# Routing stage of a fused decoder layer: token weights, placing matmuls and low halves in another order

## The reference

```python
scores = jax.nn.sigmoid(x @ gate_w.T) + bias
topk_w, topk_idx = jax.lax.top_k(scores, TOPK)                     # 4 of 16 experts
topk_w = topk_w / (jnp.sum(topk_w, axis=-1, keepdims=True) + 1e-20)
...
z = jax.nn.silu(g) * u                                             # g, u: x by Wg, Wu of each expert
out = jnp.einsum('eti,ehi->th', zw, Wd)                            # zw: z by the token's weight
out = out + jax.nn.silu(x @ Sg.T) * (x @ Su.T) @ Sd.T              # the shared expert
```

## Time and profile before

| | us |
|---|---|
| median of 3 runs | 1754.04 |
| lowest and highest | 1752.56 and 1755.8 |
| profiled execution | 1757.54 |
| its span | 1755.7 |

### The profile page before, as it was taken

The page is one execution under the profiler, slowest core; times in us unless marked ns, Lnnn a source line. Parts: engine busy times, 40 slices in busy tenths (PEclk is TensorE's granted clock), DMA queues, the critical chain, the costliest instruction groups (busy, mean ns, idle before and its releaser), DMA issues. The chain is left out here.

```text
span 1755.7 us, 39041 instructions
## 1 busy us (share of the span) xinstructions
PE 1689.7 (96%) x15461; PEld 964.6 (55%) x15461; DVE 1267.1 (72%) x2051; ACT 919.4 (52%) x1518; POOL 958.2 (55%) x875
## 2 busy tenths in 40 slices
PE   7899998899999999999999999999899999999997
PEld 4666664455555555555555555555455555455553
DVE  6778776778888888888888888888785444344445
ACT  6776674656464645455555545565643333233334
POOL 5556664556464636465555555464634555455544
PEclk9999999899999999999999999999999999999999
DMA  5431223112212314122222122131266778877658
GB/s 163 133 86 39 74 62 80 61 58 88 70 64 72 109 43 142 46 100 93 72 73 97 37 97 73 37 109 37 77 226 216 145 146 224 241 190 151 116 97 299
DMA packets 88897, 190.68 MB, mean 109 GB/s; under 512 B 14800, under 2 KB 33744, under 8 KB 86672
## 3 DMA queue, kind: packets, MB, share of 16 engines
q1 hardware_dynamic: 65232, 130.72, 22.3%
q0 software_dynamic: 22912, 57.32, 16.0%
q10 hardware_dynamic: 576, 0.14, 0.0%
HBM read 124.95 MB, written 63.21 MB: 107 GB/s over the span
## 5 line engine op out<-in xcount | busy, mean ns | idle before, releaser
L1136 POOL TENSOR_TENSOR xa_sc<-xa_sc,xa_rs 128x1024 f32<-128x1024 f32 x32 | 60.8, 1901 | 375.4 <-DVE xa_rs L1396 375.4
L1125 POOL TENSOR_TENSOR xa_xs<-xa_xs,sn 128x512 f32<-128x512 f32 x160 | 233.7, 1460 | 46.3 <-ACT xa_xs L1177 46.3
L288 PE MATMUL bank<-xhl,front_h 128*128 128x512 f16 x640 | 244.4, 382 | 11.3 <-DVE front_l L670 10.0
L289 PE MATMUL bank<-xhl,front_h 128*128 128x512 f16 x640 | 244.3, 382 | 0.0
L290 PE MATMUL bank<-xhl,front_l 128*128 128x512 f16 x640 | 244.1, 381 | 0.0
L1130 POOL TENSOR_TENSOR xa_rr<-xa_x,xa_xs 128x512 f32<-128x512 f32 x160 | 232.2, 1451 | 12.7 <-DVE xa_x L1287 0.2
L2042 POOL DMA_INDIRECT scratch_y<-raw_front,moe_to x79 | 125.3, 1585 | 149.5 <-DVE mo_zl L2096 121.5
L288 PE MATMUL bank<-out_h,xa_oh 128*128 128x512 f16 x512 | 194.8, 381 | 10.2 <-DVE xa_ol L1269 8.0
L289 PE MATMUL bank<-out_l,xa_oh 128*128 128x512 f16 x512 | 194.7, 380 | 0.0
L290 PE MATMUL bank<-out_h,xa_ol 128*128 128x512 f16 x512 | 194.5, 380 | 0.0
L1176 ACT ACTIVATE xa_xs<-bank 64x512 f32<-64x512 f32 x160 | 95.0, 593 | 139.3 <-PE bank L290 124.4
(11 more groups left out here) (320 smaller groups left out, 4668.8 us busy)
## 6 DMA issues: line engine op xcount, KB each, us to landing
xa_rawc<-in_ew SPq DMA_DIRECT2D x32, 768.0 KB, 5.4
moe_ring<-scratch_w SPq DMA_DIRECT2D x16, 1536.0 KB
scratch_w<-xa_chunk_h SPq DMA_DIRECT2D x32, 384.0 KB, 2.3
scratch_w<-xa_chunk_l SPq DMA_DIRECT2D x32, 384.0 KB, 3.3
raw_front<-in_xwq SPq DMA_DIRECT2D x8, 1024.0 KB, 7.9
raw_out<-in_xwo SPq DMA_DIRECT2D x8, 1024.0 KB, 5.3
scratch_y<-acc SPq DMA_DIRECT2D x6, 1024.0 KB, 7.8
acc<-in_x POOLq DMA_DIRECT2D x4, 1024.0 KB, 7.2
```

What stands on the lines that cost most here:

```text
L288: pe.matmul(out_ap, ah, bh, start=start and m == 0, stop=False)
L289: pe.matmul(out_ap, ah, bl, start=False, stop=False)
L1125: PO.mark(pool.tensor_tensor(xr, xr, sn[:, :].rearrange("p (a s) -> p a s", a=1) .to_broadcast([P, QT // S, S]), ALU.mult), f"sm{r}", st)
L1136: PO.mark(pool.tensor_tensor(s4, s4, rs[:, :, :].rearrange("p h (t a) -> p (h t) a", a=1) .to_broadcast([P, 16, S]), ALU.mult), "nm", st)
```

## The change

- The four operations that make `w4` move from in front of the use of the counts to behind the first four groups of comparisons, in front of `z1.0` and `z1.1`.
- TensorE's order behind `counts` was: `gu1.0`, `gu1.1`, place 0 to 3, `y0.0`, place 4 to 7, `owners`, `y0.1`, `y0.2`, `y0.3`. It becomes: `gu1.0`, `y0.0`, `y0.1`, then `gu1.1` with one placing matmul behind each of its 24 wide ones, the 8 that are left of groups 0 to 3, then `y0.2` and `y0.3` with one placing matmul of groups 4 to 7 behind each of their 12 wide ones, the 20 that are left, and `owners`. The rest (`y1.0`, `y1.1`, `turn0` and so on) is as before.
- The low halves `zl1.0` and `zl1.1` of quarter 1 are no longer made by GpSimd ahead of its wait for the list, but by VectorE behind `list` and in front of `tables`.

The number of matmuls is the same. In `front_with_places` and `back` the three products of `three_pass` are written out one by one. The diff, shortened:

```diff
--- before.py
+++ after.py
@@ -1642,14 +1642,14 @@
             assert PLACES == 8
 
             PE = Timeline(sem("ro_pe"), [], 0,
-                          ["logits"] + quad("gu", 0, IB) + ["counts"] + quad("gu", 1, IB) + several("place", *range(4)) + ["y0.0"]
-                          + several("place", *range(4, 8)) + ["owners", "y0.1", "y0.2", "y0.3", "y1.0", "y1.1", "turn0", "y1.2", "turn1", "y1.3"])
+                          ["logits"] + quad("gu", 0, IB) + ["counts", "gu1.0", "y0.0", "y0.1", "place0", "place1", "gu1.1", "place2", "place3", "y0.2", "place4",
+                                                                "y0.3"] + several("place", *range(5, 8)) + ["owners", "y1.0", "y1.1", "turn0", "y1.2", "turn1", "y1.3"])
             shared_act = [f"{w}{q}.{n}" for q in range(2) for w in ("si", "zh") for n in range(IB)]
             AC = Timeline(sem("ro_act"), [], 0, ["sig"] + shared_act + quad("y", 0, TQ) + ["y1.0", "y1.1", "xh0", "y1.2", "xh1", "y1.3"])
             DV = Timeline(sem("ro_dve"), [], 0,
-                          ["down", "chosen"] + quad("z", 0, IB) + ["w4", "slots"] + several("at", *range(4)) + quad("z", 1, IB)
-                          + several("at", *range(4, 8)) + ["own", "list", "tables", "to", "xl0", "xl1", "ws0", "ws1"])
-            PO = Timeline(sem("ro_pool"), [], 0, [x for q in range(2) for x in quad("zl", q, IB)])
+                          ["down", "chosen"] + quad("z", 0, IB) + ["slots"] + several("at", *range(4)) + ["w4"] + quad("z", 1, IB)
+                          + several("at", *range(4, 8)) + ["own", "list"] + quad("zl", 1, IB) + ["tables", "to", "xl0", "xl1", "ws0", "ws1"])
+            PO = Timeline(sem("ro_pool"), [], 0, quad("zl", 0, IB))
...
@@ -1697,7 +1697,6 @@
                     for t in range(TQ):
                         ln.rows_on_pool(pool, c, t, rows_h[c], rows_l[c])
                 low_parts(0)
-                low_parts(1)
                 pool.wait_ge(s_x, 64)
...
                 products(0)
-                then(dve.tensor_reduce(tot[:, :], top8[:, :, 0:TOPK], AX.X, ALU.add))
-                then(dve.tensor_scalar(tot[:, :], tot[:, :], 1e-20, None, ALU.add))
-                then(dve.reciprocal(rt[:, :], tot[:, :]))
-                DV.mark(dve.scalar_tensor_tensor(m.w4[:, :, :], top8[:, :, 0:TOPK], 1 / (WS * OS),
-                                                 rt[:, :].rearrange("p (t a) -> p t a", a=1).to_broadcast([P, NT, TOPK]),
-                                                 ALU.mult, ALU.mult), "w4", N0)
                 wait(dve, PE, "counts")
...
                 locate(0, 1, 2, 3)
+                then(dve.tensor_reduce(tot[:, :], top8[:, :, 0:TOPK], AX.X, ALU.add))
...
+                                                 ALU.mult, ALU.mult), "w4", N0)
                 products(1)
                 locate(4, 5, 6, 7)
...
                 DV.mark(dve.tensor_scalar(m.list[:, :], filled[:, :], -1.0, 0.0, ALU.add, ALU.max), "list", N0)
+                for n in range(IB):
+                    wait(dve, AC, f"zh1.{n}")
+                    DV.mark(dve.tensor_tensor(zl[1][:, n, :], z[:, n, :], zh[1][:, n, :], ALU.subtract), f"zl1.{n}", N0)
                 wait(dve, PE, "owners")
...
-                def place_picks(*groups):
-                    for g in groups:
+                def place(g, n):
+
+                    if n == 0:
                         wait(pe, DV, f"at{g}")
-                        j = g * NR // NT
-                        for n in range(NR):
-                            t = (g * NR + n) % NT
-                            mm = pe.matmul(bank[0][:, j * COLS:(j + 1) * COLS], at_row[g % NB][:, :, n], at_col[g % NB][:, :, n],
-                                           start=t == 0, stop=t == NT - 1)
+                    j, t = g * NR // NT, (g * NR + n) % NT
+                    mm = pe.matmul(bank[0][:, j * COLS:(j + 1) * COLS], at_row[g % NB][:, :, n], at_col[g % NB][:, :, n],
+                                   start=t == 0, stop=t == NT - 1, skip_group_check=True)
+                    if n == NR - 1:
                         PE.mark(mm, f"place{g}", N0)
 
-                def front(q, ns=range(IB)):
...
+                def places(groups, first, last):
+
+                    for m in range(first, min(last, NR * len(groups))):
+                        place(groups[m // NR], m % NR)
+
+                def front_with_places(q, n, groups):
+
+                    wait(pe, DV, f"z{q - 1}.{n}")
+                    tok, m = slice(q * QT, (q + 1) * QT), 0
+                    for u in range(2):
+                        c, o = u * FI + n * P, bank[2 + 2 * n + u]
+                        for k in range(KD):
+                            h, l = wf_h[:, k, c:c + P], wf_l[:, k, c:c + P]
+                            for w, x in ((h, xh), (l, xh), (h, xl)):
+                                mm = pe.matmul(o[:, :], w, x[:, k, tok], start=k == 0 and w is h and x is xh,
+                                               stop=k == KD - 1 and x is xl, skip_group_check=True)
+                                m += 1
+                                if m == 6 * KD:
+                                    PE.mark(mm, f"gu{q}.{n}", N0)
+                                places(groups, m - 1, m)
+                    places(groups, m, 4 * NR)
+
+                def back(q, *ts, groups=()):
                     if q == 0:
                         wait(pe, DV, "down")
-                    wait(pe, PO, f"zl{q}.1")
+                    wait(pe, DV if q else PO, f"zl{q}.1")
+                    m = 0
                     for t in ts:
                         if t >= 2:
                             wait(pe, AC, f"y{q}.{t - 2}")
                         elif q:
                             wait(pe, AC, f"y{q - 1}.{t + 2}")
                         tok = slice(t * P, (t + 1) * P)
-                        PE.mark(three_pass(pe, bank[6 + t % 2][:, :], [(zh[q % 2][:, n, tok], zl[q % 2][:, n, tok], wo_h[:, n, :], wo_l[:, n, :])
-                                                                       for n in range(IB)]), f"y{q}.{t}", N0)
+                        for n in range(IB):
+                            for a, w in ((zh, wo_h), (zh, wo_l), (zl, wo_h)):
+                                mm = pe.matmul(bank[6 + t % 2][:, :], a[q % 2][:, n, tok], w[:, n, :], start=n == 0 and a is zh and w is wo_h,
+                                               stop=n == IB - 1 and a is zl, skip_group_check=True)
+                                m += 1
+                                if m % (3 * IB) == 0:
+                                    PE.mark(mm, f"y{q}.{t}", N0)
+                                places(groups, m - 1, m)
+                    places(groups, m, 4 * NR)
...
                 PE.mark(mm, "logits", N0)
-                front(0)
+                front(0, 0)
+                front(0, 1)
...
                 PE.mark(mm, "counts", N0)
-                front(1)
-                place_picks(0, 1, 2, 3)
-                back(0, 0)
-                place_picks(4, 5, 6, 7)
+                front(1, 0)
+                back(0, 0, 1)
+                front_with_places(1, 1, range(4))
+                back(0, 2, 3, groups=range(4, 8))
                 wait(pe, DV, "own")
                 PE.mark(pe.matmul(bank[1][0:1, 0:NTILES + 2], own_h[:, :], identh[:, 0:NTILES + 2], start=True, stop=True), "owners", N0)
-                back(0, 1, 2, 3)
                 back(1, 0, 1)
                 wait(pe, DV, "z1.1")
```

19 lines of the change are left out of this document (9 added, 10 removed).

## The result

The changed kernel takes 1759.4 us (median of 8; 1757.18 to 1762.03), the kernel before, run beside it, 1755.46 us (8; 1752.56 to 1757.15). The ratio is 1.0027 with a 95% interval of 1.0017 to 1.0036: slower, by 3.0 to 6.3 us, with 4.7 us at its middle; the two medians alone differ by 3.9 us. The profiled execution took 1758.44 us, with a span of 1756.6 us.

What follows compares the result with a forecast made beforehand. TensorE, busy 1689.7 of 1755.7 us, bounds the kernel; the list comes 5.1 us later, `turn0` 3.8 later, and the expert loop moves as a block: 1754.04 + 3.8 = 1757.8 us, range 1753 to 1761.5.

Steps and rivals of the forecast that it cites:

- step 5: First gather: starts at 1337.5, rows land between 1341.5 and 1344.2; `turn0` taken at 1342.9, 3.8 us later.
- Step 1: VectorE, `w4` behind four comparison groups: `prior` still waits for GpSimd, first group 0.9 us earlier, bounds 0.5 and 1.85.
- Step 2: TensorE, placing matmuls between wide ones: each costs 0.155 us there too, since the strided moving operand can't hide.
- The first rival: Placing matmuls hide between wide ones at 0.06 us each; `turn0` 0.3 to 1.8 us later, 1755.1; chance 0.25.
- Step 3: TensorE's new order: new waits of 1 and 1.3 us, last placing matmul 5.1 us later, list at 1336.6.
- Step 4: `zl1` on VectorE behind the list: TensorE idle 2 us, `back(1,0,1)` ends 1340.5 to 1343.1; on GpSimd it held up nothing.
- the quiet stretch: Late in the trace, a gather issued at 1441.25 is through by 1445.25: 4.0 us, against 6.76 beside expert weights.
- The clock rival: TensorE's clock falls more often, between 1326 and 1332 or in the first expert tile: +6 to +9, 1761.5; chance 0.09.
- the sign of another loop: Expert loop's length differing by more than 1 us would show the forecast wrong; faster through the loop, 1751, had chance 0.08.

Runs made afterwards that it cites:

- w4_alone: Kernel before with only the four `w4` operations moved behind the fourth comparison group; ratio 1.0004 to the kernel before.
- undo_order: Changed kernel with TensorE's old order, so `w4` late and `zl1` on VectorE behind the list; ratio 0.9998 to the kernel before.
- undo_zl: Changed kernel with `zl1` back on GpSimd, `w4` late and the new order kept; ratio 1.0039 to the kernel before.
- order_alone: Kernel before with only TensorE's new order, `w4` early and `zl1` on GpSimd; ratio 1.0059 to the kernel before.
- moving_unit: Changed kernel with `at_col` laid out so that placing matmuls read the moving operand in unit step; ratio 1.0093 to the kernel before.
- weights_unit: Changed kernel with `at_row` laid out so that placing matmuls read their weights in unit step; ratio 1.0176 to the kernel before, one execution.
- zl_before_list: Changed kernel with `zl1` on VectorE in front of its wait for the last placing matmul, not behind the list; ratio 1.0013 to the kernel before.
- before_moving_unit: Kernel before with `at_col` laid out so that placing matmuls read the moving operand in unit step; ratio 1.0107 to the kernel before.
- narrow: Kernel before with `w4` late, `zl1` on VectorE, moving operand in unit step by eight operations per group; ratio 1.0033 to the kernel before.
- short_path: As the kernel before with `w4` late, `zl1` on VectorE, eight unit-step writes per group; also `z1` later, `y0` copies earlier, `y0.0` to `y0.3` between placing groups; 1.0025.

## Why the prediction was right

Forecast was slower by 3.8 us, measured +3.9 by the medians and 3.0 to 6.3 by the interval, with 4.7 at its middle. The forecast median, 1757.8, is 1.6 below the measured 1759.4 mainly because its base, 1754.04, was the median of three runs and the eight have 1755.46. The path to the list came out as reasoned, to 0.2 us at every step; that the last sum met the medians' difference is partly luck (step 5). Step by step, in us behind the counts (the prediction's times less 1307.91; those of the changed kernel less 1306.91):

| step | predicted | measured |
|---|---|---|
| first comparison group | 9.04 | 8.89 |
| TensorE's wait for it | 1 | 0.94 |
| placing matmul between wide ones | 0.155 | 0.153 |
| last wide of `gu1.1` | 17.3 | 17.2 |
| wait for `y0.0`'s copy | 1.3 | 1.28 |
| `y0.2` starts | 20.3 | 20.2 |
| group 4 | 20.6 | 20.4 |
| last placing matmul done | 27.9 | 27.8 |
| list | 28.7 | 28.7 |
| wait for `zl1` | 2 | 1.91 |
| `turn0` | 35.0 | 34.0 |

**Step 1, `w4`.** Right to 0.15 us: `more` started at once, `prior` was held by GpSimd (1.28 us instead of 0.43) and took back half of the gain. In `w4_alone` and `undo_order` it was not held, and the first group came at 8.4: the row of before showed one outcome of two. What I left out is its worth inside the new order: against `undo_zl`, which has `w4` late, `order_alone` lists 3.0 us later still in the profiles (the intervals of the two ratios overlap).

**Step 2, the placing matmuls.** Right, and its reason is shown by `moving_unit` and `weights_unit`: the moving operand with its step of 16 bytes. The Trainium skill's rule on lines of 16 bytes (SBUF — State Buffer, Door 1: The DMA port swizzle) agrees with both runs for the moving operand: 0.153 against 0.04 us. For the weights, read with the same step, the runs show no such price (a pair takes 0.37 us in either layout). No run has a step other than 16 bytes, so that it is the line and not any step is not shown. The first rival, that they hide, is out: with the strided moving operand not one pair was faster than 0.36.

**Step 3, the order.** Right, with both waits named and sized. `undo_order` shows that without this part there is no loss, and `order_alone` that it needs no other.

**Step 4, `zl1`.** Right for the changed kernel (1.91 us, half clock in 8 of the 12 wide matmuls, the last of them in part). Wrong in what it said of the side it came from: on GpSimd `zl1` "held up nothing", which held in the old order and in that execution. `undo_zl`, `order_alone` and `w4_alone` show it holding up the comparisons.

**Step 5, the gather: the mis-sized term.** I put its landing between 4.0 and 6.76 us after its start. Once the experts' weights are in, it lands in 3.6 (`zl_before_list`, `undo_zl`); in the quiet stretch I had taken as a lower bound GpSimd had also issued a scatter, at 1439.36, 1.9 us ahead of the gather. So in the changed kernel TensorE, not the gather, came last, at 34.0 instead of 35.0, and the stage accounts for 2.8 us. The prediction had the last link of the path wrong there, though 34.0 lies in the range it gave TensorE's own chain (32.6 to 35.2). The other 1.1 of the medians' 3.9 (1.9 of the 4.7) I can't place; it is small beside the width of the interval (3.3 us), and in the profiled executions the counting matmuls end anywhere from 1306.2 (`before_moving_unit`) to 1311.5 (`undo_zl`). Executions in which the clock falls in `y0.2` as well would add to it, but only one execution of the changed kernel was profiled, so that is open.

**The rivals.** The clock rival did not happen in the profiled execution, but it is real: with the same order and a longer wait it came in `order_alone` and `undo_zl`, and in `zl_before_list`, which differs from the changed kernel only in where `zl1` stands, TensorE fell to half clock within `y0.2` as well. So that the profiled execution escaped it is in part luck; I gave it 0.09. The loop kept its length: from `turn0` to the end 416.6 us before (1755.7 - 1339.14) and 415.7 after (1756.6 - 1340.95). The 1 us that I had set as the sign of another loop was too fine, as that length spreads over 4 us among the profiled executions.

## What to carry to other kernels

Ask of every wide matmul that is moved ahead of a dependency what it covered where it stood: here 30 of them stood behind the list and covered the gather, so that it cost nothing, and 18 of those were moved ahead of the list, which they delay. Interleaving a short matmul between wide ones pays only if it costs less there than by itself; here it cost 0.153 us in either place. Its recorded duration (334 ns for 83 columns, where 512 columns in unit step have 382) told beforehand that the moving operand streams slowly. And parts of a change are worth different amounts together than alone: the same two edits that moved nothing in the old order (0.9998) save the new one from twice the loss (1.0059 without them, 1.0027 with them).

## What the runs showed of the hardware

- A placing matmul whose moving operand (83 float16 columns) has a step of 16 bytes costs 0.153 us back to back, at full and at half clock, and 0.153 between wide ones at full clock. Between wide ones at half clock it costs 0.127 (`order_alone`: 0.554 for a pair, 0.427 for a wide one alone). With the moving operand in unit step it costs 0.04 between wide ones at full clock (`moving_unit`) and 0.06 to 0.07 back to back (`before_moving_unit`). The stationary operand with the step of 16 bytes adds nothing to either: its load is recorded with 144 ns (changed kernel) instead of 119 (`weights_unit`), and the pair takes 0.37 in both layouts.
- VectorE's write of float16 with a step of 166 or 256 bytes took 4.5 to 4.6 ns a number (2.99 us for 664, 4.69 us for 1024), six to seven times what the same operation takes in unit step (0.50 and 0.68).
- VectorE's operation on 83 float16 numbers with two scalars per partition (a comparison and a product) has a pitch of 0.21 us (`narrow`).
- VectorE and GpSimd hold each other up in either direction: 7.73 us for GpSimd's two subtractions where VectorE's comparisons run undisturbed, or 2.53 to 2.84 us for them and 1.45 to 1.65 for a VectorE operation of 0.5 to 0.7. Twice GpSimd's recorded start lies 0.23 us behind that of the comparison: in the kernel before GpSimd then waited, in `w4_alone` VectorE did.
- The rows of a gather of 128 rows were there 3.6 us after its start when the last load of expert weights lay 5.7 us or more behind (`zl_before_list`, `undo_zl`), and 7.1 us after it beside a load of 1.5 MB issued 2.1 us before (`short_path`).
- The same order of matmuls is granted different clocks in different executions: `w4_alone` and the kernel before have the same, and `w4_alone` was at half clock from 1321.3 to 1335.0 without a break, where the kernel before had 1.00 from 1327.3 to 1330.7.
